# Recurrent attention with a routed expert layer, one core: who computes the shift of a layer normalisation

## The chip, the cores and the metric

One core of one Trainium2 chip runs the kernel. The metric is the device time of an execution in microseconds, as the median of several runs. The five engines are TensorE (PE, matmuls and transposes), VectorE (DVE), ScalarE (ACT), GpSimd (POOL) and SyncE (SP, here only the issuer of DMAs). Each runs its own stream of instructions in order; they meet at semaphores only.

## The reference, cut to what matters

The input x has 2 batches of 2048 tokens with 256 features.

```
x = x + attn(layernorm(x))          # recurrent: chunks, a state carried from chunk to chunk
x = x + ffn(layernorm(x))           # 8 experts, the best 2 per token, 256 -> 1024 -> 256

layernorm(x) = (x - mean) / sqrt(var + 1e-5)
attn(y): v = y W_write^T; per head: reads = decayed state and masked scores times v
         return y + (alpha * reads) W_read^T
ffn(y):  probs = softmax(y gate_w^T); top 2; sum of gate * (gelu(y w1 + b1) w2 + b2)
```

Both normalisations are applied as one multiplication and one addition: with rs = (var + eps)^-0.5 and shift = -mean * rs, the normalised row is rs * x + shift. The first one is followed by a residual of its own, (1 + rs) * x + shift.

## The kernel before, in words

**Two stages.** The recurrent part walks over 16 chunks of 128 tokens, both batches at once, as a software pipeline of steps. The expert part then runs over tiles of 256 or 128 routed rows. Each engine has its own function step(n) (VectorE's from line 930, GpSimd's from 475, ScalarE's from 679, TensorE's inside its block, SP's from 388), and in step n it handles several chunks at different ages: chunk n is loaded and normalised, n-1 transposed, n-2 scored and read, n-3 projected, added as residual and normalised again, n-4 given its gate logits, n-5 ranked and sent to the rows of its experts. The order of work within a step is the order of the calls in step, written out by hand. Steps 0 to 2 are written out ahead of it with first_normalise and first_residual (lines 1196 and 1205), where VectorE does what ScalarE does later, and the last chunks behind it, mixed with the first expert tiles (from line 1259 on VectorE, 750 on ScalarE).

**Semaphores.** reached(engine, name, n) makes the engine wait until item n of the named counter is done. The counters of the two normalisations are moments, ve, rs and shift, 1 for the chunk's and 2 for the residual's.

**The two normalisations.** VectorE makes the statistics and moments (lines 881 and 789 for the chunk, 858 and 866 for the residual), mean in column 0 and variance in column 1. GpSimd turns them into rs and shift, four operations on a 128x2 tile for each: it adds epsilon (line 488), scales the mean by -1 (489), raises to the power -0.5 (491) and multiplies (493). ScalarE applies them: line 630 normalises the chunk, 675 makes its residual, 601 normalises the residual into the row that is to be sent.

**GpSimd's step** is the four operations for chunk n, the four for chunk n-3, and then four scatters for chunk n-5 (line 501, indirect DMAs of 128 rows each), which wait for the slots that VectorE computes.

**VectorE's step** is, in order: chunk_stats(n), largest(n-5), carry(n-3), moments(n), choose(n-5), chunk_low(n-1) with line 899, chunk_queries(n-1), residual(n-3) with line 851, the first split_low (line 779), residual_stats(n-3) with line 858, weigh_gates(n-5), residual_moments(n-3) with line 866, weigh_scores(n-2) with line 915, place(n-5), which ends in line 844 with the slots, logits(n-4) with line 873, and the remaining split_low.

**Weights.** The 32 pieces of the experts' weights are loaded and split during the recurrent part into a high and a low 16-bit half: ScalarE copies the high half (line 569), VectorE subtracts (line 779, 128x1024, both inputs in SBUF). PIECES gives how many belong to each step:

```
PIECES = (0, 0, 1, 3, 3, 3, 3, 3, 2, 2, 2, 2, 2, 2, 2, 2)
```

The first piece of a step is split in the middle, behind residual(n-3), and the others at the end, behind logits(n-4).

**TensorE's step** is the transposes of the chunk (line 1375), project(n-3) with line 1338, the transposes of the normalised residual (1325), values (1402), score weights (1388), rank (1362 to 1365), states (1441), expert logits (1349), reads (1421 and 1428). ScalarE copies the reads out (lines 640 and 643) ahead of the projection, and the transposed chunk in line 653.

**At the handover** VectorE turns the rows of an expert tile (1133), makes its low half (low_tile, line 1140) and splits the hidden activations (split, lines 1146 and 1148).

Of the kernel before, what the change touches and what calls it, by code (L numbers as in the profile page):

```python
# [1 line left out]

# [10 lines left out]
ALU = mybir.AluOpType  # L28
# [3 lines left out]
P = 128  # L32
B, T, D = 2, 2048, 256
# [77 lines left out]
def build(nc, x, w_write, w_read, decay, log_alpha, gate_w, experts, b1, b2, const, out):  # L111
    with ExitStack() as ctx:
        def sb(name, shape, dt=F32):
            return ctx.enter_context(nc.sbuf_tensor(name, shape, dt))
# [93 lines left out]


        small_at = [0]  # L210
        tiny = sb("tiny", [P, 188])

        def small(w, dt=F32):
            a = small_at[0]
# [3 lines left out]

        by_batch = lambda v: v.rearrange("p (b e) -> p b e", b=B)
        stats1 = by_batch(small(B * 6))  # L220
        moments1 = by_batch(small(B * 2))
        rs1, shift1, gain1 = ([small(B) for _ in range(2)] for _ in range(3))
        ve1 = small(B)
        stats2 = by_batch(small(B * 6))
# [7 lines left out]
        esum, rsum = small(B), small(B)  # L232
        slot_i = small(ROWS * B * 2, I32).rearrange("p (s w) -> p s w", s=ROWS)
        slots = by_batch(small(B * E))
        assert small_at[0] <= 188
        pick = sb("pick", [P, B, 2, E])
        picked = sb("picked", [P, B, 2, E])
        mask = sb("mask", [P, B, E], BF16)
# [61 lines left out]
        def reached(eng, name, n):  # L300

            if n >= 0:
                eng.wait_ge(S[name], n + 1)
# [160 lines left out]
        @block.gpsimd  # L464
        def _(pool):
            pool.memset(minus_half[:], -0.5).then_inc(setup_pool, 1)
            pool.memset(zcol[:], 0.0)
            pool.memset(state[:], 0.0)
            last = pool.memset(readsT[:, 0, :, :, 0:1], 0.0)
            last.then_inc(setup_pool, 1)  # L470
            pool.memset(zrow, 0.0).then_inc(setup_pool, 1)
            pool.memset(pad[:], 0.0).then_inc(setup_pool, 1)
            pool.wait_ge(setup_pool, 1)

            def step(n):

                par = n % 2
                for lag, moments, ve, rs, shift, got, mid, end, last, used, ago in (
                        (0, moments1, ve1, rs1[par], shift1[par], "moments1_done", "ve1_done", "rs1_done",
                         "shift1_done", "res_done", 1),  # L480
                        (3, moments2, ve2, rs2, shift2, "moments2_done", "ve2_done", "rs2_done", "shift2_done",
                         "xm_done", 0)):
                    if active(n, lag):

                        m = n - lag
                        reached(pool, got, m)
                        reached(pool, used, m - ago - 1)
                        pool.tensor_scalar(ve, moments[:, :, 1], EPS, None, ALU.add)  # L488
                        pool.tensor_scalar(shift, moments[:, :, 0], -1.0, None, ALU.mult).then_inc(S[mid], 1)
                        reached(pool, mid, m)  # L490
                        pool.tensor_tensor(rs, ve, minus_half[:].to_broadcast([P, B]), ALU.pow).then_inc(S[end], 1)  # L491
                        reached(pool, end, m)
                        pool.tensor_tensor(shift, shift, rs, ALU.mult).then_inc(S[last], 1)
                if active(n, 5):
                    m = n - 5
                    for name in ("token_done", "xm_done", "gates_done", "slot_i_done"):
                        reached(pool, name, m)
                    for b in range(B):
                        for k in range(2):
                            at_bk = slot_i[:, m % ROWS, 2 * b + k:2 * b + k + 1]  # L500
                            pool.indirect_dma_start(  # L501
                                out=sent, out_offset=bass.IndirectOffsetOnAxis(ap=at_bk, axis=0),
                                in_=row[:, m % ROWS, b, :], in_offset=None).then_inc(row_out[m % ROWS], 16)
                if n == 2:

                    pool.wait_ge(setup_pool, 4)
                    pool.wait_ge(setup_dve, 14)
                    pool.wait_ge(padrow_done, 1)
                    for c in range(2):
                        pool.indirect_dma_start(  # L510
                            out=sent, out_offset=bass.IndirectOffsetOnAxis(ap=padrow_i[:, c:c + 1], axis=0),
                            in_=pad[:, c, :], in_offset=None).then_inc(pad_sent, 16)

            stage_one(step, 0)

            for n in range(NCH + 2, NCH + LAG):
                step(n)

            def add(i):

                if i == 0:
                    pool.wait_ge(x1_out[0], 16 * 6)
                    pool.wait_ge(x1_out[1], 16 * 5)
                if i == NE:
                    stored(pool)
                in_tile(pool, i)
                if i > 0:
                    pool.wait_ge(added, 16 * UNIT[i])
                for u in units(i):
                    came(pool, "ybias_done", u)  # L530
                    at_u = tile_in[:, u % 8, E:E + 1].bitcast(I32)
                    pool.indirect_dma_start(  # L532
                        out=out, out_offset=bass.IndirectOffsetOnAxis(ap=at_u, axis=0),
                        in_=yout[:, u % 4], in_offset=None, compute_op=ALU.add).then_inc(added, 16)

            for i in range(NT):
                add(i)
            pool.wait_ge(added, 16 * UNIT[NT])
# [233 lines left out]
        def _(v):  # L772
# [11 lines left out]
            def moments(n):  # L784

                reached(v, "stats1_done", n)
                reached(v, "ve1_done", n - 1)
                for b in range(B):
                    last = v.bn_aggr(moments1[:, b], stats1[:, b])  # L789
                last.then_inc(S["moments1_done"], 1)  # L790

            def largest(m):

# [67 lines left out]
            def residual_moments(m):  # L861

                reached(v, "stats2_done", m)
                reached(v, "ve2_done", m - 1)
                for b in range(B):
                    last = v.bn_aggr(moments2[:, b], stats2[:, b])
                last.then_inc(S["moments2_done"], 1)

            def logits(m):

# [59 lines left out]
            def step(n):  # L930
# [22 lines left out]
                    residual(n - 3)  # L953
                for j in splits(n)[0:1]:
                    split_low(j)
                if active(n, 3):
                    residual_stats(n - 3)
                if active(n, 5):
# [6 lines left out]
                    weigh_scores(n - 2)  # L965
                if active(n, 5):
                    place(n - 5)
                if active(n, 4):
                    logits(n - 4)
                if n == NCH + 1:  # L970
# [266 lines left out]
            forget()  # L1237
            chunk_stats(1)
            moments(1)
            first_normalise(0)  # L1240
            spread_heads()
            first_residual(0)
            first_normalise(1)
            chunk_low(0)
            first_residual(1)
# [4 lines left out]
            chunk_stats(2)  # L1250
            moments(2)
            chunk_queries(0)
            mask_decay()
            weigh_scores(0)
            chunk_queries(1)
# [10 lines left out]
            residual_stats(NCH - 1)  # L1266
            residual_moments(NCH - 1)
            split(0)
            place(m)
            low_tile(1)  # L1270
            logits(m + 1)
# [321 lines left out]
```

## Time and profile before

| | |
|---|---|
| median of 3 runs | 571.51 us (568.94 to 571.64) |
| span of the profiled execution | 576.6 us |
| TensorE busy | 534.6 us, 93% |
| VectorE busy | 457.3 us, 79% |
| ScalarE busy | 332.8 us, 58% |
| GpSimd busy | 244.5 us, 42% |
| recurrent part | about the first 163 us |
| from there | handover to about 205 us, then expert tiles |

The profile is one execution. The page gives no time for it beside the span, which lies 5 us above the median of the runs; differences between two kernels are therefore worked out within the trace and then set against the median. A timeline row reads: start in us, duration in us, engine, line, operation, output <- input, count, and in brackets the idle time of the engine before it with what ended it. "Issue" in the brackets is idle time for which the trace shows no wait. A DMA_INDIRECT row on POOL is GpSimd's own work for that DMA. The time of a matmul group's end is modelled.

### The profile page before, as it was taken

Reading aid. Unit: us, or ns where it says so; the run is one execution under the profiler, and the core shown is the slowest. Engines: PE = TensorE matmul, PEld = TensorE weight load, DVE = VectorE, ACT = ScalarE, POOL = GpSimd, SP = SyncE. Lnnn points to the kernel's source line nnn. Section 1 sums busy time; section 2 is a strip of 40 time slices with the busy share of each in tenths; the row PEclk is TensorE's granted clock in tenths of the full one; section 3 lists DMA queues with packets and bytes.
Section 4 is the critical chain, followed back from the end, with each engine's and each line's share of the span. In section 5 each row is a group of like instructions: output and inputs, shape, how many; then the busy total and the mean of one; then the engine's idle time right before and its main releaser. Section 6 shows DMA issues by size and latency. Waiting matters only on the chain.

```text
span 576.6 us, 17660 instructions
## 1 busy us (share of the span) xinstructions
PE 534.6 (93%) x5246; PEld 418.7 (73%) x5246; DVE 457.3 (79%) x1408; ACT 332.8 (58%) x841; POOL 244.5 (42%) x275
## 2 busy tenths in 40 slices
PE   7799889899988888999999999999999999999991
PEld 7677777777776656777777777777777777777770
DVE  5889999999976789777887877777777887877771
ACT  5899989888744633444545444544454545444540
POOL 2426778888846532432333222333332333222333
PEclk8999999999998979999999999999999999999996
DMA  5577767667334353444444344444444433444432
GB/s 162 199 221 224 254 205 214 188 216 215 122 96 123 113 179 58 78 71 68 67 65 62 63 70 75 78 75 75 70 71 67 68 62 62 65 69 76 76 48 27
DMA packets 85097, 63.34 MB, mean 110 GB/s; under 512 B 54224, under 2 KB 77392, under 8 KB 85008
## 3 DMA queue, kind: packets, MB, share of 16 engines
q1 hardware_dynamic: 71328, 43.94, 31.0%
q0 software_dynamic: 13392, 18.27, 17.1%
q8 instruction: 49, 0.80, 0.6%
q14 instruction: 40, 0.33, 0.2%
q10 hardware_dynamic: 288, 0.00, 0.0%
HBM read 37.56 MB, written 24.62 MB: 108 GB/s over the span
## 4 chain that ended last, share of the span: by engine, by line
PE 63%; DVE 13%; POOL 8%; issue 8%; ACT 3%; SPq 1%; DMA 1%; another core or an unknown queue 0%; ACTq 0%; DVEq 0%; POOLq 0%
PE psum L1518 29%; PE psum L1533 20%; PE psum L1535 10%; POOL sent_rows L501 4%; DVE weights L779 2%; POOL tiny L491 2%; POOL tiny L488 1%; DVE arena L915 1%; SPq L429 1%; PE psum L1338 1%; DVE tiny L858 1%; DMA arena<-in_x 1%; DVE tiny L881 1%; DVE arena L1146 1%; DVE arena L851 1%
## 5 line engine op out<-in xcount | busy, mean ns | idle before, releaser
L1518 PE MATMUL psum<-arena,weights 128*128 128x256 f16 (+1 forms) x2208 | 281.4, 250 | 4.3 <-issue 4.3
L1518 PEld LDWEIGHTS psum<-arena,weights 128*128 x2208 | 188.8, 99 | 83.1 <-issue 6.6
L737 ACT ACTIVATE arena<-psum,b_cur 128x256 f32<-128x256 f32 (+1 forms) x368 | 131.7, 423 | 159.9 <-PE psum L1518 120.4
L532 POOL DMA_INDIRECT out<-arena,tile_in x71 | 115.0, 1620 | 251.6 <-DVE arena L1161 150.3
L1533 PE MATMUL psum<-weights,arena 128*128 x568 | 215.7, 381 | 2.1 <-DVE arena L1148 2.1
L1535 PE MATMUL psum<-weights,arena 128*128 x568 | 155.4, 274 | 0.0
L1148 DVE TENSOR_TENSOR arena<-arena 128x512 f16<-128x512 f32 x142 | 99.6, 701 | 4.9
L501 POOL DMA_INDIRECT sent_rows<-arena,tiny x64 | 65.3, 1021 | 27.3 <-issue 16.6
L1146 DVE CAST arena<-arena 128x512 f16<-128x512 f32 x142 | 61.8, 435 | 6.1 <-ACT arena L737 5.8
L1533 PEld LDWEIGHTS psum<-weights,arena 128*128 128x128 f16 x568 | 55.8, 98 | 8.7 <-issue 2.6
L1535 PEld LDWEIGHTS psum<-weights,arena 128*128 128x128 f16 x568 | 55.8, 98 | 4.8
L1156 DVE SCALAR_TENSOR_TENSOR arena<-psum,gate_scaled,arena 128x256 f32<-128x256 f32 x71 | 32.0, 480 | 30.0 <-PE psum L1535 25.6
L1133 DVE STREAM_TRANSPOSE tileT<-arena 128x512 f32<-128x512 f32 (+1 forms) x46 | 26.8, 583 | 34.6 <-DMA arena<-sent_rows 34.6
L584 ACT ACTIVATE arena<-tileT 128x512 f16<-128x512 f32 (+1 forms) x46 | 24.5, 533 | 31.2 <-DVE tileT L1133 29.2
L779 DVE SCALAR_TENSOR_TENSOR weights<-weights 128x1024 f16<-128x1024 f32 x32 | 38.5, 1214 | 1.8 <-ACT weights L569 1.8
L1338 PE MATMUL psum<-wrT,arena 128*128 128x256 f32 x128 | 31.7, 391 | 8.8 <-ACT arena L643 8.8
L569 ACT ACTIVATE weights<-weights 128x1024 f16<-128x1024 f32 x32 | 34.2, 1070 | 0.0
L1338 PEld LDWEIGHTS psum<-wrT,arena 128*128 128x128 f32 x128 | 23.0, 189 | 14.6 <-ACT arena L643 12.1
L747 ACT ACTIVATE arena<-arena,gate_cur 128x256 f32<-128x256 f32 x71 | 33.2, 508 | 0.0
L1161 DVE SCALAR_TENSOR_TENSOR arena<-psum,gate_scaled,arena 128x256 f32<-128x256 f32 x71 | 31.8, 477 | 0.8
L488 POOL TENSOR_SCALAR tiny<-tiny 128x2 f32<-128x2 f32 x32 | 13.5, 422 | 37.8 <-DVE tiny L789 21.1
L491 POOL TENSOR_TENSOR tiny<-tiny,minus_half 128x2 f32<-128x2 f32 x32 | 25.5, 797 | 2.7
(172 smaller groups left out, 641.8 us busy)
## 6 DMA issues: line engine op xcount, KB each, us to landing
weights<-in_experts SPq DMA_DIRECT2D x32, 512.0 KB
arena<-sent_rows SPq DMA_DIRECT2D x100, 64.0 KB
arena<-in_b SPq DMA_DIRECT2D x46, 128.0 KB
arena<-in_x SPq DMA_DIRECT2D x16, 256.0 KB, 3.7
out<-arena SPq DMA_DIRECT2D x16, 256.0 KB, 4.1
arena<-sent_rows SPq DMA_DIRECT2D x84, 32.0 KB
sent_rows<-pad SPq DMA_DIRECT2D x7, 265.0 KB
tile_in<-sent_rows SPq DMA_DIRECT2D x71, 4.5 KB
```

The lines of the kernel that those rows point to most:

```text
L491: pool.tensor_tensor(rs, ve, minus_half[:].to_broadcast([P, B]), ALU.pow).then_inc(S[end], 1)
L501: pool.indirect_dma_start(out=sent, out_offset=bass.IndirectOffsetOnAxis(ap=at_bk, axis=0), in_=row[:, m % ROWS, b, :], in_offset=None).th ...
L532: pool.indirect_dma_start(out=out, out_offset=bass.IndirectOffsetOnAxis(ap=at_u, axis=0), in_=yout[:, u % 4], in_offset=None, compute_op=A ...
L569: a.activation(halves[:, j * 2 * PIECE:j * 2 * PIECE + PIECE], weights[:, (j + AHEAD) * PIECE:(j + AHEAD + 1) * PIECE], ACT.Copy, scale=WS ...
L737: last = a.activation(act[:, g % 2, m * n:(m + 1) * n], ps_h[:, g % 2, m * n:(m + 1) * n], ACT.Gelu_apprx_tanh, scale=1.0 / WSCALE, bias=b ...
L779: v.scalar_tensor_tensor(out=halves[:, j * 2 * PIECE + PIECE:(j + 1) * 2 * PIECE], in0=weights[:, (j + AHEAD) * PIECE:(j + AHEAD + 1) * PI ...
L1146: v.tensor_copy(h_hi[:, g % 4], act[:, g % 2]).then_inc(S2["hhi_done"], 1)
L1148: v.tensor_tensor(h_lo[:, g % 4], act[:, g % 2], h_hi[:, g % 4], ALU.subtract).then_inc(S2["split_done"], 1)
L1338: last = pe.matmul(ps_proj[:, b], readsT[:, s, b, k, 0:P], wrT[:, k], start=(k == 0), stop=(k == KD - 1))
L1518: last = pe.matmul(ps_h[:, f % 2, mm * n:(mm + 1) * n], w1_of(e_of[i], k, lo, per * (f - GROUP[i]) + mm), turned[:, i % 2, part, k, 0:n], ...
L1533: pe.matmul(to, h_hi[:, z % 4, at], w2_of(e_of[t], m), start=(m == 0), stop=(m == MF - 1), skip_group_check=True)
L1535: last = pe.matmul(to[:, 0], h_lo[:, z % 4, at], w2_of(e_of[t], m)[:, 0], start=False, stop=(m == MF - 1), skip_group_check=True)
```

## The change

GpSimd keeps the epsilon addition and the power of both normalisations. The two products of mean and rs become one operation each on VectorE: chunk_shift(n) in the middle of VectorE's step, between the first split_low and residual_stats, and residual_shift(n-3) behind place(n-5) and ahead of logits(n-4). The chunk's moments get two buffers, and with them moments(n) waits for the epsilon addition of chunk n-2 in place of n-1. GpSimd's addition also waits for its own power of the chunk before. Nothing else changes its order; the small-tile buffer grows by four words.

```diff
-        moments1 = by_batch(small(B * 2))
+        moments1 = [by_batch(small(B * 2)) for _ in range(2)]
...
                         m = n - lag
                         reached(pool, got, m)
                         reached(pool, used, m - ago - 1)
-                        pool.tensor_scalar(ve, moments[:, :, 1], EPS, None, ALU.add)
-                        pool.tensor_scalar(shift, moments[:, :, 0], -1.0, None, ALU.mult).then_inc(S[mid], 1)
+                        reached(pool, end, m - 1)
+                        pool.tensor_scalar(ve, moments[:, :, 1], EPS, None, ALU.add).then_inc(S[mid], 1)
                         reached(pool, mid, m)
                         pool.tensor_tensor(rs, ve, minus_half[:].to_broadcast([P, B]), ALU.pow).then_inc(S[end], 1)
-                        reached(pool, end, m)
-                        pool.tensor_tensor(shift, shift, rs, ALU.mult).then_inc(S[last], 1)
...
                 reached(v, "stats1_done", n)
-                reached(v, "ve1_done", n - 1)
-                for b in range(B):
-                    last = v.bn_aggr(moments1[:, b], stats1[:, b])
+                reached(v, "ve1_done", n - 2)
+                for b in range(B):
+                    last = v.bn_aggr(moments1[n % 2][:, b], stats1[:, b])
                 last.then_inc(S["moments1_done"], 1)
+
+            def chunk_shift(n):
+
+                reached(v, "rs1_done", n)
+                v.scalar_tensor_tensor(out=shift1[n % 2], in0=moments1[n % 2][:, :, 0], scalar=-1.0, in1=rs1[n % 2],
+                                       op0=ALU.mult, op1=ALU.mult).then_inc(S["shift1_done"], 1)
...
+            def residual_shift(m):
+
+                reached(v, "rs2_done", m)
+                v.scalar_tensor_tensor(out=shift2, in0=moments2[:, :, 0], scalar=-1.0, in1=rs2, op0=ALU.mult,
+                                       op1=ALU.mult).then_inc(S["shift2_done"], 1)
...
                 for j in splits(n)[0:1]:
                     split_low(j)
+                if active(n, 0):
+                    chunk_shift(n)
                 if active(n, 3):
                     residual_stats(n - 3)
...
                 if active(n, 5):
                     place(n - 5)
+                if active(n, 3):
+                    residual_shift(n - 3)
                 if active(n, 4):
                     logits(n - 4)
...
             moments(1)
+            chunk_shift(0)
             first_normalise(0)
             spread_heads()
             first_residual(0)
+            chunk_shift(1)
             first_normalise(1)
...
             chunk_queries(0)
+            chunk_shift(2)
             mask_decay()
             weigh_scores(0)
...
             residual_moments(NCH - 1)
             split(0)
+            residual_shift(NCH - 1)
             place(m)
             low_tile(1)
```

## Rows read from the trace of the kernel before

**Rows 1.** The page's chain of work that ended last, its shares by line.

```profile
PE psum L1518 29%; PE psum L1533 20%; PE psum L1535 10%; POOL sent_rows L501 4%; DVE weights L779 2%; POOL tiny L491 2%; POOL tiny L488 1%; DVE arena L915 1%; SPq L429 1%; PE psum L1338 1%; DVE tiny L858 1%; DMA arena<-in_x 1%; DVE tiny L881 1%; DVE arena L1146 1%; DVE arena L851 1%
```

**Rows 2.** Busy time by stretch, core 0: us, PE, PEld, DVE, ACT, POOL, clock, DMA.

```profile
62.40:72.80 10.40, 9.22 (x113) 7.68 (x112) 10.33 (x41) 9.25 (x24) 7.88 (x12) 1.00 0.80 256
102.00:112.30 10.30, 9.22 (x117) 7.73 (x114) 9.39 (x40) 8.77 (x22) 8.62 (x13) 1.00 0.74 207
```

**Rows 3.** Timeline of POOL from 106 to 118 us: start, us, engine, line, what.

```profile
107.24 1.23 POOL L488 TENSOR_SCALAR tiny<-tiny 128x2 f32<-128x2 f32 x1
...
108.84 0.72 POOL L491 TENSOR_TENSOR tiny<-tiny,minus_half 128x2 f32<-128x2 f32 x1
...
111.29 1.14 POOL L493 TENSOR_TENSOR tiny<-tiny 128x2 f32<-128x2 f32 x1
112.60 1.08 POOL L501 DMA_INDIRECT sent_rows<-arena,tiny  x1 [0.17 <-issue]
...
117.54 1.24 POOL L488 TENSOR_SCALAR tiny<-tiny 128x2 f32<-128x2 f32 x1
```

**Rows 4.** Groups by line, 0 to 270 us: POOL lines 489 and 493.

```profile
L493 POOL TENSOR_TENSOR tiny<-tiny 128x2 f32<-128x2 f32 x32 | 13.9, 434 | 2.5
...
L489 POOL TENSOR_SCALAR tiny<-tiny 128x2 f32<-128x2 f32 x32 | 7.5, 233 | 2.0
```

**Rows 5.** Timeline of DVE, 107 to 112 us: the two weight splits.

```profile
107.17 1.22 DVE L779 SCALAR_TENSOR_TENSOR weights<-weights 128x1024 f16<-128x1024 f32 x1
...
111.16 1.22 DVE L779 SCALAR_TENSOR_TENSOR weights<-weights 128x1024 f16<-128x1024 f32 x1
```

**Rows 6.** Waits from 82 to 152 us: who for whom, total, times, longest.

```profile
ACT arena L601 <- POOL tiny L493: 6.6, 6, 1.2
...
DVE arena L851 <- PE psum L1338: 2.4, 5, 0.5
```

**Rows 7.** Timeline of DVE from 80 to 91 us, one step from slots to slots.

```profile
80.76 0.17 DVE L844 TENSOR_REDUCE tiny<-picked 128x4 int32<-128x32 f32 x1
...
80.93 1.21 DVE L779 SCALAR_TENSOR_TENSOR weights<-weights 128x1024 f16<-128x1024 f32 x1
...
84.63 0.69 DVE L899 TENSOR_TENSOR arena<-psum,arena 128x512 f16<-128x512 f32 x1 [0.25 <-issue]
...
86.56 1.22 DVE L779 SCALAR_TENSOR_TENSOR weights<-weights 128x1024 f16<-128x1024 f32 x1
87.70 0.75 DVE L858 BATCH_NORM_STATS2 tiny<-arena 128x6 f32<-128x256 f32 x2
...
90.38 0.18 DVE L844 TENSOR_REDUCE tiny<-picked 128x4 int32<-128x32 f32 x1
```

**Rows 8.** Timeline of POOL from 81 to 87 us: first scatter, then line 488.

```profile
81.75 1.35 POOL L501 DMA_INDIRECT sent_rows<-arena,tiny  x1 [0.93 <-DVE tiny L844]
...
86.97 0.89 POOL L488 TENSOR_SCALAR tiny<-tiny 128x2 f32<-128x2 f32 x1
```

**Rows 9.** Timeline of DVE at 96 us: the residual add of step 10.

```profile
96.26 0.69 DVE L851 TENSOR_TENSOR arena<-psum,arena 128x512 f32<-128x512 f32 x1 [0.46 <-PE psum L1338]
```

**Rows 10.** Timeline of DVE: slots of step 6, split of step 7, slots of step 15.

```profile
59.90 0.17 DVE L844 TENSOR_REDUCE tiny<-picked 128x4 int32<-128x32 f32 x1
...
66.52 1.21 DVE L779 SCALAR_TENSOR_TENSOR weights<-weights 128x1024 f16<-128x1024 f32 x1
...
151.72 0.18 DVE L844 TENSOR_REDUCE tiny<-picked 128x4 int32<-128x32 f32 x1
```

**Rows 11.** Timelines of POOL at 56 and 182 us and of DVE at 182 us.

```profile
56.30 1.59 POOL L491 TENSOR_TENSOR tiny<-tiny,minus_half 128x2 f32<-128x2 f32 x1
...
182.27 0.72 POOL L491 TENSOR_TENSOR tiny<-tiny,minus_half 128x2 f32<-128x2 f32 x1
...
182.68 0.67 DVE L1140 TENSOR_TENSOR arena<-tileT,arena 128x512 f16<-128x512 f32 x1
```

**Rows 12.** Timeline of DVE at 21 us: the first weight split.

```profile
21.16 1.23 DVE L779 SCALAR_TENSOR_TENSOR weights<-weights 128x1024 f16<-128x1024 f32 x1 [1.83 <-ACT weights L569]
```

More of the change, by code:

```diff
@@ L210, in build @@
         small_at = [0]
-        tiny = sb("tiny", [P, 188])
+        tiny = sb("tiny", [P, 192])
         def small(w, dt=F32):
@@ L234, in build @@
         slots = by_batch(small(B * E))
-        assert small_at[0] <= 188
+        assert small_at[0] <= 192
         pick = sb("pick", [P, B, 2, E])
@@ L477, in step @@
                 par = n % 2
[L478 to L482, printed above, removed]
+                for lag, moments, ve, rs, got, mid, end, used, ago in (
+                        (0, moments1[par], ve1, rs1[par], "moments1_done", "ve1_done", "rs1_done", "res_done", 1),
+                        (3, moments2, ve2, rs2, "moments2_done", "ve2_done", "rs2_done", "xm_done", 0)):
                     if active(n, lag):
```

## The prediction

> **What bounds the kernel now.** I began with the chain that ended last, by line [rows 1]. The reader should see that GpSimd stands on it in spite of its small busy share: the row scatters of line 501 and the two small operations of lines 488 and 491 lie there together, beside VectorE's weight split of line 779. GpSimd is touched by this change only in the recurrent part (the first 160 us or so), so that part alone was read closely.
>
> Next came busy time by stretch [rows 2]. In the step from 62.4 us VectorE is busy 10.33 of 10.40 us: it is the bound while three pieces of the experts' weights are split per step. In the step from 102.0 us it is busy 9.39 of 10.30, with two pieces per step; something else sets the pace there.
>
> GpSimd's own order of events shows what [rows 3]. It never waits in such a step. But its first epsilon addition takes 1.23 us and its second shift product 1.14 us, where the neighbour of the first, the same kind of operation, takes 0.23 us on average [rows 4]. VectorE's rows beside them [rows 5] give the reason: line 779 (two SBUF inputs, 1.22 us) starts just before each and ends within 0.1 us of its end. An operation of GpSimd that begins while line 779 runs is held until that ends; 0.08 us of it are then left (107.17 + 1.22 against 107.24 + 1.23). The second hold delays ScalarE's normalise of line 601 by up to 1.2 us, six times in this stretch [rows 6], and through the projection VectorE's residual add in five steps [rows 6]. So the present cycle is split, held shift, normalise, reads, projection, residual, split: 10.30 us.
>
> **What the change removes.** Two operations per normalisation leave GpSimd: the scaling of line 489 (0.23 us) and the product of line 493 (0.43 us on average with its holds) [rows 4], with 0.07 us of gap each (in rows 3, from 108.47 to 108.84 stand one line 489 and two gaps). The second product no longer meets line 779, because VectorE makes that shift ahead of its split. ScalarE's wait of rows 6 then goes. Taken alone this is a gain of up to 1 us in most two-piece steps.
>
> A rule bears on this. The Trainium skill (GPSIMD Engine Reference, Engine selection) says to put elementwise arithmetic on VectorE. By it the step would follow the shorter queue of GpSimd and the change would gain; that is the second rival below.
>
> **What it adds, and the new wait.** VectorE gets two small operations per step. Their price is the spacing of its small operations: from line 844 to line 779, with one copy between, 0.17 us [rows 7], so 0.09 each. The price that matters is their place. The chunk's shift stands in the middle of VectorE's step and waits for GpSimd's power; GpSimd comes to that power only after the four scatters of the step before; and these wait for the slots that VectorE computes at the end of that step. Behind the waiting shift stand, on VectorE, the residual statistics, gates, moments, score weights and the next slots; TensorE's reads wait for the score weights. That is a closed loop which the kernel before doesn't have, as there VectorE never waits for GpSimd in a step.
>
> Its length, counted from S, the start of line 844: where GpSimd waited for the slots, its first scatter started at S + 0.99 and line 488 at S + 6.21 [rows 7, 8]. The second shift pushes the split behind the slots by 0.09, and the first scatter reads during that split, so I take S + 6.30.
>
> *Two-piece steps (9 to 15).* VectorE's first split starts at S + 5.80 [rows 7]; the 0.09 vanishes in the wait of line 899 (0.25 us, same rows). It runs to S + 7.02, so line 488 at 6.30 is held and ends at 7.10. Gap 0.07, power 0.72 (7.89, line 491 in rows 3), 0.07 to reach VectorE (taken as the gap), shift 0.09: statistics at 8.05. From there to the next S are 2.68 us (87.70 to 90.38, same rows): period 10.73. In five of the seven steps the residual add waited 0.46 us more [rows 6, 9]. The split then runs 6.26 to 7.48. If line 488 is held again the period is 11.19; if it slips in first, the power is held instead (of line 488's 0.23 us 0.08 were left after the hold, so about 0.14 pass before it bites, and 0.58 of the power is left) and the period is 10.90. I take the middle, 11.05. Sum: 2 x 10.73 + 5 x 11.05 = 76.7 us against 80.76 to 151.72 = 71.0 us [rows 7, 10]: **+5.7 us**. Bounds: +4.1 (7 x 10.73) to +7.4 (7 x 11.19).
>
> *Three-piece steps (6 to 8).* VectorE is full; the split starts 6.62 us after S [rows 10], now 6.71. Line 488 at 6.30 is free, the power starts at 6.60, 0.11 before the split. If it gets its operands in that time the step only grows by two shifts: 6.71 + 1.14 + 0.09 + 2.68 = 10.62 against 10.43, +0.19, three times +0.6. If it is held: 7.93 + 0.58 + 0.07 + 0.09 + 2.68 = 11.35, three times +2.8. For the first: a power that had begun 0.41 us before a two-input operation of VectorE was not lengthened; against it: one begun inside a split took 1.59 us [rows 11]. The order of the starts decides, so I take **+0.6** and keep +2.8 as bound.
>
> The holds are where the rule matters most. The Trainium skill (GPSIMD Engine Reference, Specifications) names VectorE instructions with two SBUF inputs or in a two-port mode as those that contend for the shared SBUF interfaces. The trace agrees for line 779 [rows 3, 5]. By that rule the new shift is such an instruction too, which speaks against the change; it runs while GpSimd waits for the slots or has its operands, so the sum stays the same.
>
> *The rest.* Steps 3 to 5 have no scatters: the shifts cost between nothing and 3 x 0.19; **+0.3**. At the start line 489 no longer precedes the first power (-0.3), but a shift stands ahead of the second normalise (+0.2): **-0.1**. The third chunk's shift waits on VectorE for epsilon and power, at most 0.23 + 0.07 + 0.72 = 1.0 us; it is hidden by the 1.83 us in which VectorE waits for ScalarE's first weight copy [rows 12], without which it would cost all of that. In the handover to the experts the last residual shift stands ahead of the slots and of the second tile's low half: the power starts at 182.27 and takes 0.72 us, and that low half, line 1140, starts at 182.68 [rows 11]; VectorE would wait up to 0.7 us with both behind it. I count 0, since tile 0 has four groups of matmuls to run before that low half is needed; 0.7 is the bound. The second moments buffer and the looser wait behind it (n - 2 in place of n - 1) I cost at nothing, since the addition waited for is a step old either way; so is the power for which GpSimd's addition now waits.
>
> Sum: 5.7 + 0.6 + 0.3 - 0.1 = **+6.5 us** in the profiled execution, whose span is 576.6 us, 5 us above the median of the runs. The steps are the same in both, so I add it to 571.5: **578.0 us**.
>
> **Rivals.**
> *The split does not hold GpSimd in the loop* (or line 488 and the power both find gaps). Period 6.30 + 0.23 + 0.07 + 0.72 + 0.07 + 0.09 + 2.68 = 10.16, seven steps 71.1, +0.2; with the rest about +1.0: 572.5. For it: the new phases aren't in the trace. Against: line 779 starts before 6.30 in all my cases.
> *The wait is not the bound; GpSimd's shorter queue wins.* VectorE alone gives 9.62 - 0.25 + 0.18 = 9.55 [rows 7], seven steps -4.1, with the rest -3.3: 568.2. It decides only if the power ends before VectorE reaches the shift at S + 6.94. Unheld it ends at 7.32 and reaches VectorE at 7.39, so the four scatters would have to be 0.45 us shorter in all. For it stands the gain at line 601; against it, that from the first scatter to line 488 it took 4.94 us in rows 3 and 5.22 in rows 8, no less.
> *Every power or epsilon addition is held*, in three-piece steps too: +2.8 + 7.4 + 0.2 = 10.4, 582.0. For it: 0.11 us of margin is thin.
>
> **How the numbers follow.** Forecast 0.54, all held 0.14, no hold 0.22, GpSimd's queue 0.10. A measurement of this kernel can tell about 0.5% (2.9 us) from no change. The forecast with its bounds (575 to 582) and the all-held case are slower: 0.68; the no-hold case is the same: 0.22; the last faster: 0.10. The range leaves out the fast rival and little of the all-held case: 570.5 to 582.5.
>
> **What would show it.** A wait of VectorE's chunk shift for GpSimd's power, about 1 us in each of steps 9 to 15; steps of 10.7 to 11.2 us there, and 10.6 in steps 6 to 8 (11.3 if the power is held); GpSimd waiting for line 844 before each first scatter, as in rows 8, and line 601 no longer waiting for GpSimd. Wrong if the shift's wait is under 0.3 us in the two-piece steps, or if these are 10.1 us or shorter.

## The result and the profile after

The changed kernel takes **578.12 us** (median of 4 runs, 576.37 to 580.42), the kernel before in the same comparison 570.23 us (4 runs, 567.43 to 571.64): ratio 1.0146, 95% interval 1.01 to 1.0192. It is 7.9 us slower. The prediction was 578.0 us in a range of 570.5 to 582.5, and 0.68 for slower.

The profiled execution of the changed kernel has a time of 577.96 us and a span of 576.2 us, so 1.8 us lie outside the span. The span of the kernel before, 576.6 us, is no shorter, though its median is 7.9 us lower: its profiled execution was not a typical one (with the same 1.8 us outside its span it would have taken 578.4 us, an estimate). A second profile of it (the first experiment below) has a span of 567.1 us, and what follows is read against that one where it says so.

**The wait.** The waits of the changed kernel from 82 to 157 us (who for whom: total, times, longest), which answer to [rows 6]:

```profile
POOL sent_rows L482 <- DVE tiny L831: 10.7, 7, 1.5
...
ACT arena L621 <- PE psum L1429: 6.8, 7, 2.2
PE psum L1422 <- DVE arena L908: 6.4, 7, 1.1
...
ACT arena L582 <- DVE tiny L859: 5.9, 6, 1.0
DVE tiny L776 <- POOL tiny L474: 4.6, 5, 0.9
```

Line 776 is the chunk's shift, 474 GpSimd's power, 482 the scatters (before 501), 831 the slots (before 844), 859 the residual's shift, 908 the score weights (before 915), 1422 TensorE's reads. The loop that the prediction names can be read off: VectorE waits for GpSimd's power, GpSimd for VectorE's slots. TensorE waits for the score weights behind it, and ScalarE's copy of the reads for TensorE.

**One turn of the loop.** Timeline of VectorE in the changed kernel, which answers to [rows 5, 7]: first a three-piece step, then a two-piece step.

```profile
72.08 0.18 DVE L831 TENSOR_REDUCE tiny<-picked 128x4 int32<-128x32 f32 x1
...
78.76 1.21 DVE L760 SCALAR_TENSOR_TENSOR weights<-weights 128x1024 f16<-128x1024 f32 x1
79.89 0.15 DVE L776 SCALAR_TENSOR_TENSOR tiny<-tiny 128x2 f32<-128x2 f32 x1
...
82.64 0.18 DVE L831 TENSOR_REDUCE tiny<-picked 128x4 int32<-128x32 f32 x1
...
103.89 0.18 DVE L831 TENSOR_REDUCE tiny<-picked 128x4 int32<-128x32 f32 x1
103.99 0.15 DVE L859 SCALAR_TENSOR_TENSOR tiny<-tiny 128x2 f32<-128x2 f32 x1
...
107.51 0.69 DVE L892 TENSOR_TENSOR arena<-psum,arena 128x512 f16<-128x512 f32 x1
...
109.44 1.21 DVE L760 SCALAR_TENSOR_TENSOR weights<-weights 128x1024 f16<-128x1024 f32 x1
111.57 0.16 DVE L776 SCALAR_TENSOR_TENSOR tiny<-tiny 128x2 f32<-128x2 f32 x1 [0.92 <-POOL tiny L474]
...
114.33 0.18 DVE L831 TENSOR_REDUCE tiny<-picked 128x4 int32<-128x32 f32 x1
```

And GpSimd beside it, which answers to [rows 3, 8]:

```profile
78.31 0.24 POOL L472 TENSOR_SCALAR tiny<-tiny 128x2 f32<-128x2 f32 x1
78.64 0.72 POOL L474 TENSOR_TENSOR tiny<-tiny,minus_half 128x2 f32<-128x2 f32 x1
...
104.89 1.41 POOL L482 DMA_INDIRECT sent_rows<-arena,tiny  x1 [1.52 <-DVE tiny L831]
...
109.14 0.96 POOL L482 DMA_INDIRECT sent_rows<-arena,tiny  x1 [0.30 <-issue]
110.12 0.61 POOL L472 TENSOR_SCALAR tiny<-tiny 128x2 f32<-128x2 f32 x1
110.81 0.72 POOL L474 TENSOR_TENSOR tiny<-tiny,minus_half 128x2 f32<-128x2 f32 x1
```

With S = 103.89 the first scatter starts at S + 1.00, epsilon at S + 6.23, 0.68 us after the start of the split of line 760; it is held until 110.73, just past the split's end at 110.65. The power follows at once, the shift at S + 7.68, and 2.76 us later the next slots: 10.44 us. In the three-piece step epsilon and power are free (0.24 and 0.72 us), the power having started 0.12 us ahead of the split: 10.56 us.

**TensorE's clock.** Busy time by stretch of the changed kernel (us; PE, PEld, DVE, ACT, POOL; granted clock; DMA): the start, the recurrent part, and three two-piece steps of it.

```profile
20.00:30.00 10.00, 8.38 (x103) 6.62 (x100) 7.79 (x22) 7.06 (x17) 1.88 (x4) 0.90 0.25 84
...
60.00:160.00 100.00, 89.93 (x1054) 75.46 (x1054) 92.01 (x386) 84.05 (x211) 60.45 (x76) 0.97 0.65 197
93.20:104.00 10.80, 10.54 (x117) 8.89 (x114) 9.53 (x42) 8.69 (x21) 6.18 (x8) 0.84 0.64 183
103.89:114.33 10.44, 9.15 (x115) 7.72 (x113) 9.45 (x42) 9.09 (x24) 6.55 (x8) 0.99 0.75 219
114.50:125.50 11.00, 10.79 (x120) 9.18 (x118) 9.57 (x43) 8.68 (x22) 6.18 (x8) 0.86 0.58 187
```

Of the seven two-piece steps five last 10.43 or 10.44 us; the two others, 10.82 and 10.98 us, are those in which the granted clock is 0.84 and 0.86 in the stretches shown, which run nearly from slots to slots; that is a mean of the two levels (2.4 GHz and 1.2 GHz). TensorE idles 1.1 us behind the score weights just before both, but it does so before three steps at full clock as well, so this idle time alone does not decide. In the two longer steps the shift does not wait: VectorE has waited 1.2 and 1.4 us ahead of the split (0.9 and 0.5 of it for ScalarE's copy of the transposed chunk), the split starts only at S + 6.94 and S + 7.09, and the power is done before it ends.

**Where the time came from**, by the start of the slots' last operation of steps 5, 8 and 15, in us:

| stretch | before, first profile | before, second profile | after | after less second | predicted |
|---|---|---|---|---|---|
| start to slots of step 5 | 49.49 | 49.33 | 50.60 | +1.3 | +0.2 |
| steps 6 to 8 | 31.27 | 31.26 | 32.04 | +0.8 | +0.6 |
| steps 9 to 15 | 70.96 | 67.72 | 73.99 | +6.3 | +5.7 |
| the rest of the span | 424.9 | 418.8 | 419.6 | +0.8 | 0 |
| span | 576.6 | 567.1 | 576.2 | +9.1 | +6.5 |

The two spans compared differ by 9.1 us, the medians of the runs by 7.9: with one profile on each side, a row of the table can be off by a microsecond or so.

### The profile page after: what moved, and what is told of

Read it like the earlier page. It is cut to its first block, busy times and chain, and to the rows that moved or that the text cites. A ratio compares the mean times of both kernels' runs of the same rounds, so it can differ in the third digit from the quotient of the medians.

```text
span 576.2 us, 17628 instructions
## 1 busy us (share of the span) xinstructions
PE 534.9 (93%) x5246; PEld 420.4 (73%) x5246; DVE 459.5 (80%) x1440; ACT 334.0 (58%) x841; POOL 219.5 (38%) x211
## 4 chain that ended last, share of the span: by engine, by line
PE 62%; DVE 19%; issue 7%; POOL 6%; DMA 2%; ACT 1%; SPq 1%; DVEq 0%; POOLq 0%; ACTq 0%
PE psum L1519 29%; PE psum L1534 19%; PE psum L1536 10%; POOL sent_rows L482 4%; DVE arena L908 3%; DVE weights L760 2%; PE psum L1429 2%; PE psum L1422 2%; DMA arena<-sent_rows 1%; DVE tiny L845 1%; POOL tiny L474 1%; DVE arena L1143 1%; DVE arena L838 1%; DVE tiny L874 1%; DVE arena L919 1%
## 5 line engine op out<-in xcount | busy, mean ns | idle before, releaser
L1519 PE MATMUL psum<-arena,weights 128*128 128x256 f16 (+1 forms) x2208 | 278.4, 248 | 1.1 <-DVE arena L1137 0.7
L482 POOL DMA_INDIRECT sent_rows<-arena,tiny x64 | 67.8, 1059 | 39.3 <-DVE tiny L831 24.4
L1422 PE MATMUL psum<-arena 128*64 128x128 f32 x256 | 20.2, 305 | 12.3 <-DVE arena L908 12.3
L472 POOL TENSOR_SCALAR tiny<-tiny 128x2 f32<-128x2 f32 x32 | 9.2, 286 | 58.1 <-DVE tiny L853 32.6
```

The source lines that it names most:

```text
L482: pool.indirect_dma_start(out=sent, out_offset=bass.IndirectOffsetOnAxis(ap=at_bk, axis=0), in_=row[:, m % ROWS, b, :], in_offset=None).th ...
L1519: last = pe.matmul(ps_h[:, f % 2, mm * n:(mm + 1) * n], w1_of(e_of[i], k, lo, per * (f - GROUP[i]) + mm), turned[:, i % 2, part, k, 0:n], ...
```

## The experiments

They ran in three sessions, each on one chip with the kernel before beside it: the first four in the first, where the kernel before took 568.8 us, the next four in the second (577.07 us), the last three in the third (579.16 us). The first two sessions ran on the same chip, so the 8.3 us between them come neither from the kernel nor from another chip. Only ratios to the kernel before of the same session are therefore compared; most expectations below that are given in microseconds had the first level in mind. The theory: the chunk's shift, waiting in the middle of VectorE's step, closes a loop through GpSimd, whose length is the scatters, the hold and the power. Rivals: the residual's shift or the handover costs the time; or the hold is all of it.

**before_again**: the kernel before, without an edit.

> The kernel before, unchanged, for a second profile of it. Theory (closed loop): up to the slots of step 15 it takes 151.7 us again, within 0.5, with GpSimd never idle in steps 10 to 13, because that part is a repeating pattern; its span is 567 to 570 us, so that the 576.6 us of the first profile are explained by the handover after step 15. Rival (the recurrent part itself varies from run to run by several us): the slots of step 15 come at another time, by 2 us or more.

568.93 us (one run), span 567.1. The slots of step 15 come at 148.31 us and not at 151.7: the rival held, the recurrent part itself varies. One step of its timeline of VectorE:

```profile
99.61 0.18 DVE L844 TENSOR_REDUCE tiny<-picked 128x4 int32<-128x32 f32 x1
...
103.61 0.69 DVE L899 TENSOR_TENSOR arena<-psum,arena 128x512 f16<-128x512 f32 x1 [0.36 <-ACT arena L653]
104.94 0.68 DVE L851 TENSOR_TENSOR arena<-psum,arena 128x512 f32<-128x512 f32 x1
105.54 1.21 DVE L779 SCALAR_TENSOR_TENSOR weights<-weights 128x1024 f16<-128x1024 f32 x1
...
109.35 0.18 DVE L844 TENSOR_REDUCE tiny<-picked 128x4 int32<-128x32 f32 x1
```

Two-piece steps take 9.74 us here, not the 10.30 of [rows 2], and line 851 doesn't wait, although GpSimd's product is held just the same and line 601 waits as in [rows 6]:

```profile
106.18 0.66 POOL L488 TENSOR_SCALAR tiny<-tiny 128x2 f32<-128x2 f32 x1
...
109.66 1.13 POOL L493 TENSOR_TENSOR tiny<-tiny 128x2 f32<-128x2 f32 x1
```

So the kernel before has at least two rhythms. In the faster one the hold of GpSimd's product costs a step at most about 0.4 us, if the 9.35 us of residual_only below, where there is no such product, are taken for the step without it.

**chunk_only**: VectorE makes the chunk's shift, GpSimd the residual's again.

```diff
+                        (3, moments2, ve2, rs2, "moments2_done", "ve2_done", "rs2_done", "xm_done", 0,
+                         shift2, "shift2_done")):
...
-                if active(n, 3):
-                    residual_shift(n - 3)
...
-            residual_shift(NCH - 1)
```

> VectorE makes the chunk's shift; GpSimd keeps both operations of the residual's shift. Theory (the cost is the chunk shift's place in a loop of slots, scatters, power, shift): the loop is still closed and GpSimd's queue is longer than in the changed kernel by 0.29 + 0.28 us in the second half, which is off the loop unless its last product is held by the split behind the slots and ScalarE's normalise waits for it again. Steps 9 to 15 take 10.4 to 10.9 us, the time is 577 to 582 us, slower than before by 1 to 2%. Rival (the cost comes from the residual's shift on VectorE and the handover): near 570 us.

576.35 us (574.2 to 578.47), ratio 1.0121, interval 1.009 to 1.0152. Steps 9 to 15 take 10.38 to 11.68 us. The median is just below the 577 to 582 expected. The chunk's shift alone brings most of the loss (1.2%, where the whole change cost 1.5%).

**residual_only**: the reverse; GpSimd makes the chunk's shift, VectorE the residual's.

```diff
+                        (0, moments1[par], ve1, rs1[par], "moments1_done", "ve1_done", "rs1_done", "res_done", 1,
+                         shift1[par], "shift1_done"),
...
-                if active(n, 0):
-                    chunk_shift(n)
...
-            chunk_shift(0)
...
-            chunk_shift(1)
...
-            chunk_shift(2)
```

> VectorE makes the residual's shift; GpSimd keeps the chunk's. Theory: no wait of VectorE for GpSimd in the middle of the step, ScalarE's normalise no longer waits for a held product, VectorE sets the pace: steps 9 to 15 take 9.5 to 9.8 us in place of 10.1 on average, 2.4 to 4.5 us less in all; the time is 566 to 569 us. The handover still has the wait of 0.6 us for the last power. Rival (moving any product to VectorE costs by the two-input hold or by VectorE's own time): 572 us or more.

566.99 us (12 runs, 565.83 to 571.4), ratio 0.9966, interval 0.9942 to 0.9989. Steps 10 to 15 take 9.35 or 9.36 us and VectorE waits for nothing in them. This half of the change is a small gain beside the kernel before of 568.8 us.

**late_shift**: both shifts stay on VectorE; the chunk's moves from ahead of the residual's statistics to behind the residual's moments, three calls later.

```diff
-                if active(n, 0):
-                    chunk_shift(n)
...
                     residual_moments(n - 3)
+                if active(n, 0):
+                    chunk_shift(n)
```

> The changed kernel with the chunk's shift behind the residual's moments, about 1.05 us later on VectorE, so that statistics, gates and moments run while the power is made. Theory (closed loop): in the changed kernel the power reaches VectorE 7.7 us after the start of the slots' last operation, and VectorE was there 0.9 us earlier; it now arrives at about 7.7, the wait goes to 0.1 or less, and the steps shrink from 10.44 to 9.6 us, by 5 to 6 us over steps 9 to 15, until ScalarE or TensorE is late; the time is 568 to 573 us. Rival (the loss isn't in that wait but in the two operations themselves or in TensorE's clock): within 1 us of the changed kernel's 578.

568.92 us (12 runs, 567.5 to 570.44), ratio 1.0002, interval 0.9984 to 1.0019. Its waits from 81 to 148 us have GpSimd's for the slots, and none of VectorE for the power:

```profile
POOL sent_rows L482 <- DVE tiny L831: 11.6, 7, 1.7
...
ACT arena L621 <- PE psum L1429: 4.2, 7, 0.6
```

The two-piece steps take 9.49 or 9.50 us. With the same operations on the same engines the whole loss is gone: the place is the cause, not the work.

**changed_again**: the changed kernel, in the second session.

> The changed kernel, unchanged, as the control of this group. Theory: steps 9 to 15 take 10.44 us or more again, with the steps above that being those in which TensorE's granted clock is below 1.0; the time is 576 to 580 us. Rival (its pattern, too, differs from run to run, as that of the kernel before does between 9.74 and 10.30 us a step): steps of another length at full clock.

583.75 us (583.17 to 585.43), ratio 1.0113, interval 1.0077 to 1.0148. The time lies above the 576 to 580 expected, but the kernel before is 8.3 us slower there too. Steps 10 to 15 take 10.44 or 10.45 us. Of the longer ones step 9 (10.85) has a granted clock of 0.86. Step 8 (11.58) has 0.98, and its cause is another: GpSimd's first scatter (line 482, at 74.84) takes 2.54 us there in place of 1.41. Epsilon starts 1.13 us later, the split holds it as in the two-piece steps (0.61 us), and the shift comes at S + 8.81 in place of S + 7.68: the 1.13 us come through the whole loop.

**no_mid_split**: in the changed kernel, from step 8 on, the split in the middle of the step goes to its end.

```diff
-                for j in splits(n)[0:1]:
+                for j in splits(n)[0:1] if n < 8 else ():
                     split_low(j)
...
-                for j in splits(n)[1:]:
+                for j in splits(n)[1:] if n < 8 else splits(n):
                     split_low(j)
```

> The changed kernel with the mid-step weight split moved to the end of the step, from step 8 on, so that no operation of VectorE with two large SBUF inputs runs when GpSimd comes to the chunk's epsilon addition. VectorE's work per step is the same. Theory (the split holds GpSimd inside the loop): the epsilon addition goes from 0.6 to 0.23 us and the step from 10.44 to 10.07 us; VectorE still waits, now about 0.6 us; the time is 2.5 us below the changed kernel's (more where fewer steps lose TensorE clock). Rival (nothing is held, the loop is scatters and power alone, or VectorE's own time bounds it): steps of 10.44 us and the same time.

582.5 us (581.28 to 584.71), ratio 1.0105, interval 1.0065 to 1.0144. Timeline of GpSimd; the step's slots came at 112.59:

```profile
113.59 1.41 POOL L482 DMA_INDIRECT sent_rows<-arena,tiny  x1 [1.53 <-DVE tiny L831]
...
118.82 0.24 POOL L472 TENSOR_SCALAR tiny<-tiny 128x2 f32<-128x2 f32 x1
119.14 0.72 POOL L474 TENSOR_TENSOR tiny<-tiny,minus_half 128x2 f32<-128x2 f32 x1
```

Epsilon starts at S + 6.23 as before, and takes 0.24 us in place of 0.61. The steps take 10.07 us in place of 10.44, exactly the hold; the wait remains, with 0.5 us:

```profile
DVE tiny L776 <- POOL tiny L474: 3.8, 7, 0.5
```

Steps 9 to 15 sum to 70.49 against 73.50 us in changed_again, but the medians differ by 1.25 us only, and their ranges overlap. In its profile step 17, at the handover, takes 14.38 against 12.63 us. That step is long with the session, whatever the kernel: 9.9 to 10.3 us in the four profiles of the first session and in the first of the changed kernel, 11.0 in the first of the kernel before, 12.6 to 14.7 in all seven of the second and third. What makes it so was not found. So the hold is one part of the loop's length, and what it gives in the steps was not seen in full at the end.

**power_twice**: GpSimd raises the chunk's variance to the power twice, the first time into a spare tile.

```diff
+                        if lag == 0:
+                            pool.tensor_tensor(rs_extra, ve, minus_half[:].to_broadcast([P, B]),
+                                               ALU.pow).then_inc(S["extra_done"], 1)
+                            reached(pool, "extra_done", m)
```

> The changed kernel with the chunk's power made a second time on GpSimd, into a spare tile, ahead of the real one: 0.72 us and a gap, 0.80 us more in GpSimd's queue in each step. Theory (closed loop through GpSimd): every one of steps 9 to 15 grows by the full 0.80 us, to 11.2 us, steps 6 to 8 to about 11.3; with the start 9 to 10 us more, 586 to 590 us. Rival (GpSimd has slack and the wait is set by something else): less than 3 us more.

595.57 us (593.79 to 598.34), ratio 1.0335, interval 1.0288 to 1.0383; 11.8 us above changed_again. Timeline of GpSimd in three of its steps, of 11.21, 11.90 and 11.54 us (line 476 is the extra power, 479 the real one):

```profile
91.29 0.62 POOL L473 TENSOR_SCALAR tiny<-tiny 128x2 f32<-128x2 f32 x1
91.99 0.72 POOL L476 TENSOR_TENSOR tiny<-tiny,minus_half 128x2 f32<-128x2 f32 x1
92.79 0.69 POOL L479 TENSOR_TENSOR tiny<-tiny,minus_half 128x2 f32<-128x2 f32 x1
...
102.51 0.23 POOL L473 TENSOR_SCALAR tiny<-tiny 128x2 f32<-128x2 f32 x1
102.82 1.79 POOL L476 TENSOR_TENSOR tiny<-tiny,minus_half 128x2 f32<-128x2 f32 x1
...
114.73 0.72 POOL L476 TENSOR_TENSOR tiny<-tiny,minus_half 128x2 f32<-128x2 f32 x1
115.53 1.40 POOL L479 TENSOR_TENSOR tiny<-tiny,minus_half 128x2 f32<-128x2 f32 x1
```

Three of the seven two-piece steps take 11.21 us, at a granted clock of 1.00: 0.77 more than 10.44. In them epsilon is held as before (0.62 us at 91.29), and what is added on GpSimd is one unheld power with its gap (0.69 + 0.08). It comes out in the period one for one, as it must if the loop goes through it. The other four take 11.38 to 11.90 us at 0.83 to 0.87. In them VectorE's split (line 765, 1.22 us) comes later, epsilon slips in ahead of it, and a power is held in its place: 1.79 us where it starts together with the split (both at 102.82), 1.40 us where it starts 0.37 us into it (115.53, the split at 115.16). This is part of why the whole loss is 11.8 us and not the 9 to 10 expected.

**residual_mixed**: as residual_only, but GpSimd also makes the residual's shift of chunks 0 to 2 and of the last one, so that the start and the handover are nearly those of the kernel before.

```diff
+                        if lag == 3:
+                            shift, last = (shift2, "shift2_done") if m < 3 or m == NCH - 1 else (None, None)
...
-                if active(n, 3):
+                if active(n, 3) and n >= 6:
                     residual_shift(n - 3)
...
-            residual_shift(NCH - 1)
```

> The version with only the residual's shift on VectorE, but GpSimd makes it for the first three chunks and for the last one, so that VectorE does not wait for the last power at the handover. Theory: the handover wait of VectorE (0.7 us, with the slots and the second tile's low half behind it) goes; tile 0 has slack there, so the time falls by 0 to 0.7 us against 567.0: 566 to 567.5 us, below the kernel before. Rival (the first steps or the handover are what gave the gain): 568.5 us or more.

571.77 us (6 runs, 570.96 to 573.5), ratio 0.9908, interval 0.9875 to 0.9941: faster than both kernels. The expectation, 566 to 567.5 us, was set at the level of the first session and can't be read against this time; the ratio is better than residual_only's 0.9966 in that session, hence the next group.

The last three ran once more beside each other.

**before_third**, **residual_only_2** and **residual_mixed_2**: the kernel before, residual_only and residual_mixed, unchanged.

> The kernel before, unchanged, a third time. It settles which of the two patterns of the two-piece steps is the usual one: steps of 9.74 us with line 851 not waiting, as in its second profile, or of 10.30 us, as in its first. Expected: 9.74 in most of the steps 9 to 15.

> residual_only once more, on one chip with residual_mixed. If the residual's shift on VectorE is the gain (steps 6 to 15 of 10.5 and 9.35 us, no wait of VectorE for GpSimd in the loop), its ratio to the kernel before lies between 0.992 and 0.998 again. If the first value was chance, the interval holds 1.

> residual_mixed once more, beside residual_only. Both have the same steps from 3 to 15; they differ at the start and in the handover only. If the ends of the pipeline are worth something, it is faster than residual_only by 1 us or more on the same chip; if its 0.9908 came from the other chip, both ratios are equal within 0.2%.

before_third: 580.27 us, one run. Its steps 9 to 15 take 9.64, 9.75, 11.98, 10.63, 9.64, 10.39 and 10.39 us: neither rhythm is the only one, and my expectation held for three steps of seven. Two of its stretches, slots to slots:

```profile
91.14:100.89 9.75, 8.96 (x112) 7.53 (x109) 9.31 (x41) 8.34 (x22) 8.06 (x13) 1.00 0.76 218
...
112.87:123.50 10.63, 10.54 (x116) 9.02 (x114) 9.41 (x40) 8.51 (x21) 8.09 (x13) 0.84 0.55 157
```

residual_only_2: 578.06 us (12 runs, 576.43 to 581.38), ratio 0.9981, interval 0.9956 to 1.0006, which holds 1. residual_mixed_2: 572.91 us (6 runs, 571.55 to 574.2), ratio 0.9891, interval 0.9852 to 0.9931. The gain of the mixed version came back, and no run of it overlaps with one of residual_only: 5.1 us between medians in one session. The steps 6 to 15 of both are nearly alike (98.16 and 97.28 us); in the profiles 5.8 us more lie between the slots of step 15 and the last slots (148.07 to 200.74 against 146.69 to 193.59), and 0.5 us before the slots of step 5. The profiled execution of residual_only_2 was the slowest of its twelve, so 5.8 may be too much for a typical one. So the ends of the pipeline count in these two sessions; whether they do at the level of the first was not run. The one pair of profiles points at the handover, but which end it is, and by what wait, was not told apart. The recurrent part of residual_mixed_2, by stretch:

```profile
60.00:160.00 100.00, 93.86 (x1152) 78.44 (x1150) 97.38 (x415) 86.64 (x217) 72.00 (x99) 1.00 0.66 203
```

VectorE is busy 97.38 us of these 100, against 92.01 in the changed kernel: it is the bound again, and the loop is gone.

## Why the prediction was right, and where its terms were off

**The cause** was as predicted, and the time nearly to the microsecond, the latter by luck: the predicted growth of 6.5 us was 1.4 short of the measured 7.9, and the base of 571.5 us lay 1.3 above the 570.23 of the comparison. The cause is a closed loop from VectorE's slots over four scatters, epsilon and power to the shift that waits in the middle of VectorE's step. late_shift takes the wait away without taking work away, and the loss goes; chunk_only has the loss without the residual's shift; power_twice lengthens the loop by what it adds. For the residual's shift the forecast of a gain was also right in kind (residual_only 0.9966 in the first session; in the third its interval holds 1).

**Steps 9 to 15: +6.3 for +5.7, by two errors against each other.** The period is 10.44 and not 10.73. The step that failed is "Split starts at S + 5.80": I let line 899 keep its wait of 0.25 us and the 0.09 of the new shift vanish in it. In the run, ScalarE gets the residual's shift at about S + 0.25 (line 859 at 103.99, 0.15 us) where GpSimd's held product ended at S + 1.44 (109.66 + 1.13 in the second profile of before, slots at 109.35). Line 892, which waited in the kernel before for ScalarE's copy behind that normalise, then has no wait at all in the steps at full clock, starts at S + 3.62, and the split at S + 5.55. The hold ends 0.25 us earlier, and with small differences the period is 0.29 shorter. The second split of terms, five steps at 11.05 for a waiting residual add, fell too: line 838, that add, waits in none of these steps. The two longer steps are those with TensorE's lower clock, which the sum had no term for.

The other error is the base. I took 71.0 us for the seven steps from the one profile; the second shows 67.72, the third (before_third) 72.4. Against the first profile the growth is 3.0 us, below the bound of 4.1 that I had given. I had seen that this execution lay 5 us above the median and wrote "The steps are the same in both". That sentence is wrong: 3.2 of the 9.5 us between the two profiles of before are in these steps, 3.0 in the handover, and the rest in the expert tiles. The growth of these steps came out nearly right because the old steps, taken 3.2 us too long, and the new ones, taken 2.7 us too long, nearly cancel.

**Steps 6 to 8: +0.8 for +0.6**, 10.56 us in two of the three for the predicted 10.62. The power started 0.12 us ahead of the split, predicted 0.11, and was not held. The first of the three took 10.92. The bound of +2.8, and with it the all-held rival, falls.

**Start and steps 3 to 5: +1.3 for +0.2.** The third chunk's shift waits 0.50 us for the power, and the cover that I named was there: VectorE's wait for the first weight copy fell from 1.6 us (second profile of before) to 0.58. What I did not name stands between the two: the score weights, for which TensorE waits 3.2 us at once (1.7 before). But no_mid_split, whose program is the same up to step 7, has the same waits (0.50 and 3.2 us) and its slots of step 5 at 49.05 us, 0.3 ahead of the kernel before. So the waits by themselves cost nothing there, and the +1.3 goes with TensorE's clock, told below.

**Handover: +0.8 for 0.** VectorE waits 0.62 us there for the power, near the 0.7 given as bound. One profile on each side does not settle whether this wait is the 0.8. My reason for counting 0, that the first tile has slack, is not shown either: in the third session taking the residual's shift out of both ends gained 5.1 us.

**The rivals.** No hold, 10.16 us a step: the hold is there, and no_mid_split shows the period without it, 10.07. GpSimd's shorter queue (VectorE alone 9.55 a step): this is what late_shift (9.50) and residual_only (9.35) reach once the loop is open. It is wrong for the change as made. The rule behind it, elementwise arithmetic to VectorE (the Trainium skill, GPSIMD Engine Reference, Engine selection), so held for the residual's product in the first session and failed for the chunk's: what decided was not the engine but what stands before and behind the operation.

**Signs.** The wait of the shift was forecast as about 1 us in seven steps and is 0.9 us in five. Line 601 (now 582) was to wait for GpSimd no longer: it doesn't, yet it waits up to 1.0 us for VectorE's shift, which comes behind the loop.

## What to carry to other kernels

An operation moved to the engine that consumes its result brings a wait with it into that engine's order: before it is moved, follow what it waits for back until the chain ends or returns to the same engine. If it returns, the period cannot be shorter than the loop, and putting the operation a few calls later can win back all of the loss (here the ratio went from 1.0146 to 1.0002) at no cost. And take a base for differences from more than one profile when the profiled execution's span lies off the median.

## What the runs showed of the hardware that was not expected

**TensorE's clock at the start.** In the stretch from 20 to 30 us the granted clock is 0.90 in the changed kernel, and 1.00 in all three profiles of the kernel before. The same stretch in no_mid_split, whose program is that of the changed kernel up to step 7:

```profile
20.00:30.00 10.00, 8.18 (x118) 6.61 (x116) 9.25 (x23) 8.60 (x21) 1.88 (x4) 1.00 0.47 152
```

Its slots of step 5 start at 49.05 us, against 50.60 (clock 0.90) and 52.35 in changed_again (0.83): three executions of the same instructions up to there, with the same waits of 0.50 us for the third chunk's power and 3.2 us for the score weights. Over all thirteen profiles: the seven with 1.00 in that stretch, power_twice aside (50.62, also 1.00, with its longer loop), have these slots at 49.05 to 49.91 us; the five with 0.83 to 0.90 at 50.15 to 52.65 us. Of these five three have the chunk's shift at the start, and two (residual_only and residual_mixed) have not. So this term goes with the clock, not with the 0.50 us of the shift's wait; TensorE's longest wait for the score weights there was 3.2, 3.2, 2.4, 2.5 and 2.5 us in the five, and 1.3 to 3.2 us in the others. The ranges overlap: a long wait goes with the lower clock, but doesn't decide alone, and what does stays open.

**The hold is by the order of starts.** GpSimd's addition on 128x2 elements that begins 0.68 us into VectorE's 128x1024 operation with both inputs in SBUF ends 0.08 us after it. A power (0.72 us alone) that begins with that operation takes 1.79 us, and one that begins 0.37 us into it 1.40; they end 0.57 and 0.55 us after it, near the 0.58 that the prediction had estimated. One that begins 0.12 us ahead is not lengthened (0.72), and the operation of VectorE beside it takes its usual 1.21 us: neither of the two holds the other.
